# VectorE adds a head's scaled output straight into x

## The reference, cut to what matters

```python
q = (hidden_states @ Wq).reshape(B, S, N_HEADS, D_KV)
k = (hidden_states @ Wk).reshape(B, S, N_HEADS, D_KV)
v = (hidden_states @ Wv).reshape(B, S, N_HEADS, D_KV)
scores = jnp.einsum('bqhd,bkhd->bhqk', q, k) * (1.0 / math.sqrt(D_KV)) + bias
attn = jax.nn.softmax(scores, axis=-1)
ctx = jnp.einsum('bhqk,bkhd->bqhd', attn, v).reshape(B, S, N_HEADS * D_KV)
return ctx @ Wo
...
x = _layernorm(x + _L0_attn_ref(x, ...), axis=-1)
```

## Time and profile before

| | us |
|---|---|
| median of 3 runs | 1892.05 |
| lowest and highest run | 1890.16, 1894.46 |
| the profiled execution's own time | 1890.6 |
| its span, first to last instruction | 1888.9 |
| attention, start to about | 810 |
| add_heads to add_heads of an ordinary step | 12.09 |

### The profile page before, as it was taken

One profiled execution on the slowest core, in us unless ns is written; L12 is line 12 of the kernel. 1 busy time (PEld: TensorE's weight loads), 2 busy tenths in 40 slices (PEclk: granted clock), 3 DMA queues, 4 the chain that ended last, 5 costly groups with the idle time before them and its releaser, 6 DMA issues. The chain is left out here.

```text
span 1888.9 us, 39520 instructions
## 1 busy us (share of the span) xinstructions
PE 1630.0 (86%) x13672; PEld 1240.6 (66%) x13672; DVE 1381.6 (73%) x3843; ACT 1186.4 (63%) x2767; POOL 699.9 (37%) x665
## 2 busy tenths in 40 slices
PE   8999999999999999938676879999899989923871
PEld 6666666666666666627563458887788868822761
DVE  6888888888888888876566767776677755577324
ACT  6888888888888888835455656663566534501333
POOL 0222222112222222207456049993599921000772
PEclk9999999999999999958897889999999999955985
DMA  7000000000000000046551000000000000031544
GB/s 250 2 2 2 2 2 2 2 2 2 2 2 2 2 2 2 22 84 121 103 125 57 1 1 1 1 1 1 1 1 1 1 4 2 1 112 52 143 75 99
DMA packets 64039, 60.88 MB, mean 32 GB/s; under 512 B 10938, under 2 KB 53924, under 8 KB 63716
## 3 DMA queue, kind: packets, MB, share of 16 engines
q1 hardware_dynamic: 51380, 40.72, 7.2%
q0 software_dynamic: 10384, 16.59, 5.4%
q10 hardware_dynamic: 2080, 1.05, 0.2%
HBM read 39.60 MB, written 18.73 MB: 31 GB/s over the span
## 5 line engine op out<-in xcount | busy, mean ns | idle before, releaser
L463 ACT ACTIVATE prob<-prob,negmax 128x512 f32<-128x512 f32 x512 | 368.5, 721 | 52.0 <-DVE negmax L574 51.9
L201 POOL TENSOR_TENSOR x<-x,scaled 128x512 f32<-128x512 f32 x126 | 161.7, 1283 | 634.3 <-DVE scaled L595 625.2
L574 DVE CUSTOM_DVE_ANT_0 prob<-score_ps,bias 128x512 f32<-128x512 f32 x512 | 336.5, 685 | 6.9 <-PE score_ps L273 1.9
L313 PE MATMUL work_ps<-probT,val 128*64 128x512 f32 x1024 | 233.8, 598 | 0.3 <-DVE scaled L595 0.3
L273 PE MATMUL score_ps<-k,q 64*128 64x512 f32 x1536 | 229.6, 415 | 3.6 <-DVE negmax L574 3.6
L582 DVE COPY probT<-turn_ps 128x512 f32<-128x512 f32 x254 | 174.5, 687 | 65.6 <-PE turn_ps L297 63.3
L297 PEld LDWEIGHTS turn_ps<-ident,prob 64*128 64x128 f32 x4064 | 162.0, 139 | 86.1 <-ACT prob L463 52.8
L448 ACT COPY probT<-turn_ps 128x512 f32<-128x512 f32 x254 | 147.9, 582 | 72.0 <-PE turn_ps L297 72.0
L297 PE MATMUL turn_ps<-ident,prob 64*128 64x64 f32 x4064 | 176.2, 225 | 1.8 <-ACT prob L463 1.2
L273 PEld LDWEIGHTS score_ps<-k,q 64*128 64x128 f32 x1536 | 134.5, 187 | 28.4 <-DVE k L558 2.5
L313 PEld LDWEIGHTS work_ps<-probT,val 128*64 128x64 f32 x1024 | 67.8, 136 | 114.3 <-issue 109.1
(11 more groups left out here) (525 smaller groups left out, 4098.7 us busy)
## 6 DMA issues: line engine op xcount, KB each, us to landing
ew<-L_ffn_fc_weight SPq DMA_DIRECT2D x32, 256.0 KB, 3.2
bias<-bias_line SPq DMA_DIRECT2D x16, 448.0 KB, 9.2
mid_rows<-row SPq DMA_DIRECT2D x40, 128.5 KB
last_rows<-row SPq DMA_DIRECT2D x40, 64.0 KB
rows_dram<-qk SPq DMA_DIRECT2D x1, 2304.0 KB, 9.8
acc_dram<-zero POOLq DMA_DIRECT2D x1, 2048.0 KB, 13.6
out<-x SPq DMA_DIRECT2D x4, 512.0 KB, 3.2
x_rows<-x SPq DMA_DIRECT2D x2, 512.0 KB
```

Source lines behind the costliest of these rows:

```text
L201: pool.tensor_tensor(mine, mine, scaled[a][:, :, :], ALU.add).then_inc(added, 1)
L313: mm = pe.matmul(work[0][head(a), :], val[p // 2 % 2][:, c, p % 2 * 2 + a, :], probT[:, c, a, :], start=(c == 0), stop=(c == QT - 1))
L463: act.activation(mine, mine, ACT.Exp, bias=negmax[p % 2][:, i, a:a + 1], scale=-1.0, accum_out=total[p % 4][:, i, a:a + 1]).then_inc(exp_d ...
L574: dve.tensor_tensor_reduce(prob[p % 2][a][:, i, :], score_ps[i % 2][a][:, :], bias[:, h, first:first + SEQ][:, ::-1], -1.0, 3.0e38, ALU.ad ...
```

## The change

`scale_head` no longer writes a buffer. For each of the four tiles of the batch it issues one SCALAR_TENSOR_TENSOR on DVE: bank tile times 1/sum plus x tile, into x. POOL's loop of additions is gone with its semaphore `added`; what waited for `added` waits for `scaled_ready`, which the fourth of the operations sets. The second head of a pair waits for the first one's `scaled_ready`, since both update the same tiles. The waits of `scale_head` for `added` go, and two waits for the load of x move from POOL to DVE.

```diff
@@ block.gpsimd
-            pool.wait_ge(first_x_in, 16)
-            for p in range(STEPS - 1):
-                if p == PAIRS:
-                    pool.wait_ge(x_in, 16)
-                mine = x[:, batch_of(p) * QT:(batch_of(p) + 1) * QT, :]
-                for a in range(2):
-                    pool.wait_ge(scaled_ready, 2 * p + a + 1)
-                    if p or a:
-                        pool.wait_ge(added, 2 * p + a)
-                    pool.tensor_tensor(mine, mine, scaled[a][:, :, :], ALU.add).then_inc(added, 1)
-            pool.wait_ge(added, HEADS * BATCH - 2)
@@ scale_head(p, a)
-                    if p >= 1:
-                        dve.wait_ge(added, 2 * (p - 1) + a + 1)
-                    dve.tensor_tensor(scaled[a][:, :, :], work[a][:, :].rearrange("p (t d) -> p t d", t=QT),
-                                      inv[p % 4][:, :, a:a + 1].to_broadcast([P, QT, D]), ALU.mult).then_inc(scaled_ready, 1)
+                    if p % PAIRS == 0:
+                        dve.wait_ge(x_in if p else first_x_in, 16)
+                    if p or a:
+                        dve.wait_ge(scaled_ready, 2 * p + a)
+                    for i in range(QT):
+                        t = QT * batch_of(p) + i
+                        mm = dve.scalar_tensor_tensor(x[:, t, :], work[a][:, tile_of(i)], inv[p % 4][:, i, a:a + 1], x[:, t, :], ALU.mult, ALU.add)
+                    mm.then_inc(scaled_ready, 1)
@@ look_in_step(s)
-                        dve.wait_ge(added, 2 * PAIRS * (t // QT + 1))
+                        dve.wait_ge(scaled_ready, 2 * PAIRS * (t // QT + 1))
@@ before the last pair's sums
-            dve.wait_ge(added, 2 * LAST)
+            dve.wait_ge(scaled_ready, 2 * LAST)
```

More of the change, by code:

```diff
@@ L124, in attention @@
         names = ("score_done", "scored", "exp_done", "inv_ready", "turn_done", "turned_by_act", "turned_by_dve", "ctx_done", "ctx_ready",
-                 "val_done", "val_ready", "q_done", "q_hi", "q_lo", "k_done", "k_hi", "k_lo", "x_turned", "x_hi", "x_lo", "sum_done", "scaled_ready", "added")
+                 "val_done", "val_ready", "q_done", "q_hi", "q_lo", "k_done", "k_hi", "k_lo", "x_turned", "x_hi", "x_lo", "sum_done", "scaled_ready")
         (score_done, scored, exp_done, inv_ready, turn_done, turned_by_act, turned_by_dve, ctx_done, ctx_ready,
-         val_done, val_ready, q_done, q_hi, q_lo, k_done, k_hi, k_lo, x_turned, x_hi, x_lo, sum_done, scaled_ready, added) = (core.sem(n) for n in names)
+         val_done, val_ready, q_done, q_hi, q_lo, k_done, k_hi, k_lo, x_turned, x_hi, x_lo, sum_done, scaled_ready) = (core.sem(n) for n in names)
         line_ps = [score_ps[1][c][0:HEADS, :] for c in range(2)]
```

## The result

The changed kernel takes 1909.19 us (median of 4 runs, 1905.00 to 1910.91) where the kernel before took 1891.11 (4 runs, 1889.90 to 1894.46): a ratio of 1.0084 with a 95% interval of 1.0069 to 1.0099. Measured again later, with more runs, it was 1.0078, 1.0065 to 1.0091. The forecast was 13.4 us or 0.7% slower; the two medians are 18.1 us and 14.5 us apart.

The account below looks back on a forecast made before the run. PE was taken to bound the kernel. 62 steps at 0.21 us (13.0) plus 0.4 us at attention's end gave 13.4 us on a base of 1892.05: 1905.5 us, 0.7% slower, range 1896.5 to 1913.

Parts of the forecast that it names:

- PE sets the pace, POOL is off the path: In attention PE is always busy and nobody waits for POOL; removing its 126 additions of 1.28 us is worth nothing.
- The pitch of 0.26 us: DVE's new operations start 0.26 us apart, read from L687; one head costs 0.43 us more, a step 0.86.
- the threshold of 0.23: Start-to-start time of DVE's new operations below which PE waits in no ordinary step; rival "same", about 1892.3 us, chance 0.07.
- Place A: The bank: context waits until head 0's scaling has read it; 0.42 us later against 0.34 slack, 0.08 us late.
- Place B: The exponentials: PE's turn(s, 0) waits for the last one; 0.86 us later against 0.65 slack, 0.21 us late.
- the name in brackets: The profile put PE's 0.81 us idle before turn(s, 0) down to ACT; disbelieved, as ACT had been done for 0.65 us.
- The two don't add up: Delays of 0.08 and 0.21 us count from the same scale_head start; the later holds, step 12.09 to 12.30 us.
- The neighbour that bounded the pitch from above: Twenty L638 on DVE, with two per-token operands, give at most 0.31 us from start to start.
- the rival with the higher pitch: DVE becomes the bound: at 0.31 us an operation, steps cost 37.8 us, total 1930.3; chance 0.09 for over 1912.
- POOL's traffic had slowed somebody: Rival "faster": POOL's additions slow other engines' operations in attention; it would have to bring more than 13 us; chance 0.02.
- The end of attention: The last scaled pair has no cover: context starts 0.42 us later and PE with it, plus 0.4 us.
- the last step's turn: Last of the 62 turns following scale_head of pairs 0 to 61, each counted 0.21 us late.

Follow-up runs that it names:

- no_additions: Changed kernel with both heads scaled by the wide operation again and all additions before the last pair's left out; ratio 0.9989 to the kernel before, step 12.09 us.
- narrow_pool_adds: Kernel before, POOL's additions and buffers kept, each head's scaling cut into four 128x128 operations; ratio 1.0088, step 12.31 us.
- head0_narrow: Changed kernel with four narrow operations for head 0 only; head 1 scaled wide into its buffer, its addition left out; ratio 1.0026 to before, step 12.18 us.
- head1_later: Changed kernel with scale_head of head 1 moved behind the inversion, into DVE's idle gap; ratio 1.0027 to the kernel before, step 12.18 us.
- head1_thrice: Kernel before with head 1's wide scaling repeated twice into spare buffers, in front of the real one; ratio 1.0186, step 12.63 us.
- head1_narrow: Changed kernel with four narrow operations for head 1 only; head 0 scaled wide into its buffer, its addition left out; ratio 0.9996 to before, step 12.09 us.
- head1_twice: Kernel before with head 1's wide scaling repeated once into a spare buffer, in front of the real one; ratio 1.0000, step 12.09 us.
- no_pool_refit: Changed kernel with head 0 scaled wide, its addition and head 1's narrow operations moved behind the inversion; ratio 0.9998 to before, step 12.09 us.

## Why the prediction was right

- *PE sets the pace, POOL is off the path.* Shown by no_additions.
- *The pitch of 0.26 us*, from the start of one operation to the start of the next. Held: (1.13 − 0.34) / 3 = 0.26 in the step above. It was taken from eight instances of the same instruction elsewhere in the program. The Trainium skill's price (Vector Engine (DVE) Microarchitecture Reference, § 5.2 Measured stream behaviour on trn2) gives an estimate of 0.21 us for 128 columns, below the threshold of 0.23, and would have made the steps free. The measurement decides against it for these operations: 0.26 us in the changed kernel and in narrow_pool_adds.
- *Place A, slack 0.34 us.* A delay of 0.08 us was forecast; head0_narrow and head1_later show 0.09.
- *Place B, slack 0.65 us.* Measured as 0.66 by head1_thrice. To distrust the name in brackets and to compare times was the decisive step of the reading. Over 60 steps the loss is 0.22 us a step, where 0.21 was forecast.
- *The two don't add up.* Forecast 12.30 us, measured 12.30; a sum would have been 12.38.
- *The neighbour that bounded the pitch from above was no bound of the pitch.* The prediction took 0.31 us from twenty L638 in 6.14 us. After, the same twenty take 5.17 us, with nothing changed in them:

```profile
810.19 5.17 DVE L631 TENSOR_SCALAR x<-x,norm_inv,norm_shift 128x128 f32<-128x128 f32 x20
...
L631 DVE TENSOR_SCALAR x<-x,norm_inv,norm_shift x22: 294/335/345, 810.2 to 821.4; 128x128 f32<-128x128 f32 x22
```

  One of them had been blocked by an addition of POOL (below). It served as an end of a range only, so nothing but the price of the rival with the higher pitch was wrong.
- *"POOL's traffic had slowed somebody" was dismissed from too few rows.* The score at 400.28, taken as one outside POOL's additions, lasts until 400.97 and overlaps them, and at the end of attention POOL did hold up a DVE operation for about 1 us (the one just named). It cost nothing: the last 48 matmuls for the logits start 6.45 us after the last `ctxT` copy before (804.84) and 6.46 us after it in no_additions (805.72).
- *The end of attention was mis-sized.* The term was 0.21 us for the last step's turn and 0.4 for the rest. From copy to copy of `ctxT`, the first 60 steps took 742.20 − 729.11 = 13.1 us more, and the last three intervals 1.5 us more (14.6 − 13.1) where about 0.8 was forecast for them. These three are 12.31, 10.33 and 6.72 us where 12.09, 9.45 and 6.28 stood: 0.22, 0.88 and 0.44 more, and the forecast had 0.21, 0.21 and 0.4. So it is the last step's turn that was mis-sized. What was overlooked is a third place. In the last step ACT loads a table behind the last exponential and copies the transposes only after that. Before:

```profile
786.04 0.69 DVE L595 TENSOR_TENSOR scaled<-work_ps,inv 128x512 f32<-128x512 f32 x1
...
790.02 1.28 ACT L758 ACT_TABLE_LOAD   x1
...
791.43 0.57 ACT L448 COPY probT<-turn_ps 128x512 f32<-128x512 f32 x1
...
792.04 0.58 PEld L297 LDWEIGHTS turn_ps<-ident,prob 64*128 64x128 f32 x16 [0.59 <-ACT probT L448]
```

  After:

```profile
798.40 1.12 DVE L588 SCALAR_TENSOR_TENSOR x<-work_ps,inv,x 128x128 f32<-128x128 f32 x4
...
803.25 1.28 ACT L751 ACT_TABLE_LOAD   x1
...
804.65 0.57 ACT L437 COPY probT<-turn_ps 128x512 f32<-128x512 f32 x1
...
805.27 0.57 PEld L286 LDWEIGHTS turn_ps<-ident,prob 64*128 64x128 f32 x16 [0.91 <-ACT probT L437]
```

  From scale_head of head 0 to the copy it is 5.39 us before and 6.25 after, and PE's next turn starts 0.04 and 0.05 us behind the copy's end. All 0.86 us are on the path there, since ACT's chain of exponential, table and copy had no slack, whatever PE had. The other kernels bear this out. The same interval, the one before the last, grows by all that is put in front of the last exponential: by 0.43 us in head1_narrow, 0.44 in head0_narrow, 0.60 in head1_twice and 1.20 in head1_thrice. In no_pool_refit, where the exponentials come earlier, it shrinks to 9.17 us.
- *The rest of the distance to the first medians* (18.1 us against 14.6 in attention) is not explained by the argument, which says nothing of the later layers. It is of the size by which they scatter (up to 7 us between profiles); the second measurement gives 14.5.

## What to carry to other kernels

An engine that is 14% idle has no slack of 14%: for each thing that it hands over, take the time between arrival and use from the timeline, compare the work added in front of it with that, and put new work behind the last tight handover, in front of an idle gap. Do this for the last step of a loop by itself: its slack can be another one (none here, where 0.65 us stood in the others). Before trusting the name of a releaser, look whether the waiting engine started right behind it (0.05 us here) or long after. A fusion that cuts one 128x512 operation into four of 128x128 pays for it (0.43 us each time here), and has to save that much on the engine that waits.

## What the runs showed of the hardware

A DVE operation that reads and writes SBUF alone took 1 us longer while POOL added two SBUF operands. In the kernel before, two overlapping rows at the end of attention:

```profile
796.15 1.40 POOL L201 TENSOR_TENSOR x<-x,scaled 128x512 f32<-128x512 f32 x1
...
796.33 1.31 DVE L638 TENSOR_SCALAR x<-x,norm_inv,norm_shift 128x128 f32<-128x128 f32 x1
```

It took 1.31 us where its like take 0.34, and ended at 797.64, 0.09 us after POOL's at 797.55; POOL's own took 1.40 us, not 1.28. In after, without POOL's additions, the longest of the 22 takes 0.345 us. The Trainium skill (SBUF — State Buffer, § Who interferes with whom) says that a DVE operation in a two-port mode and one of GpSimd exclude each other for a whole instruction, and that DVE operations with at most one SBUF input outside those modes do not contend. The traces are in line with both: the scores and scalings that read the bank ran beside POOL's additions at their usual length (the scalings 0.69 us with and without), and no_additions won nothing by taking these away. Whether the operation that was held up ran in such a mode no run shows.

Start to start, four operations of 128x128 with a per-token operand out of the bank take 0.26 us each, whether they multiply alone (narrow_pool_adds) or multiply and add a third tile (the change).
